# A hybrid layer on one core: K and Q left unnormalised, their norms folded into per-token factors

## The reference, cut to what matters

```
mixed = silu(causal_conv4(x @ w_qkv));  q, k, v = split(mixed)      # 16 heads of q, k; 32 of v
q = q * rsqrt(sum(q*q) + 1e-6) * 128 ** -0.5
k = k * rsqrt(sum(k*k) + 1e-6)
state = state * exp(g_t)                                            # per head, 128 x 128
delta = (v_t - k_t @ state) * beta_t
state = state + outer(k_t, delta);   out_t = q_t @ state
core = norm_w * (out * rsqrt(mean(out*out) + 1e-6)) * silu(z);      result = core @ w_out
```

## Time and profile before

| | |
|---|---|
| median of 3 runs | 4429.54 us (4429.43 to 4431.3) |
| the profiled execution, its time | 4427.73 us |
| its span, first to last instruction | 4426.0 us |
| mean granted clock of PE | 0.984 |
| busy, share of the span | PE 96%, DVE 77%, ACT 52%, POOL 10% |

### The profile page before, as it was taken

One profiled execution on the slowest core, in us unless ns is written; L12 is line 12 of the kernel. 1 busy time (PEld: TensorE's weight loads), 2 busy tenths in 40 slices (PEclk: granted clock), 3 DMA queues, 4 the chain that ended last, 5 costly groups with the idle time before them and its releaser, 6 DMA issues. The chain is left out here.

```text
span 4426.0 us, 80007 instructions
## 1 busy us (share of the span) xinstructions
PE 4253.2 (96%) x29877; PEld 2612.2 (59%) x29877; DVE 3409.0 (77%) x8579; ACT 2317.5 (52%) x4857; POOL 433.1 (10%) x342
## 2 busy tenths in 40 slices
PE   7899999999999999999999999998699999999898
PEld 4566666666666666666666666666344444444443
DVE  5888888888888888887888888786345989898950
ACT  4555555555555555555555555554244545564542
POOL 1111111111111111111111111110000000000000
PEclk9999999999999999999999999999899999999999
DMA  2111111111111112111111110100203445454520
GB/s 73 41 37 37 32 39 32 32 35 37 32 39 32 34 33 70 44 34 32 37 33 34 42 32 30 37 30 11 90 1 99 149 140 161 147 162 136 174 83 10
DMA packets 202405, 263.32 MB, mean 59 GB/s; under 512 B 18175, under 2 KB 101379, under 8 KB 202019
## 3 DMA queue, kind: packets, MB, share of 16 engines
q1 hardware_dynamic: 202018, 258.20, 18.3%
HBM read 249.24 MB, written 8.91 MB: 58 GB/s over the span
## 5 line engine op out<-in xcount | busy, mean ns | idle before, releaser
L455 PE MATMUL bank<-xnT,w_qkv 128*128 128x512 f32 x2048 | 928.2, 596 | 4.1 <-ACT raw L738 3.4
L455 PEld LDWEIGHTS bank<-xnT,w_qkv 128*128 128x128 f32 x2048 | 374.9, 192 | 403.9 <-issue 385.2
L1028 DVE SCALAR_TENSOR_TENSOR conv<-raw,conv_w,conv 128x1024 f32<-128x1024 f32 x384 | 495.4, 1290 | 125.8 <-ACT conv L715 116.6
L568 PE MATMUL bank<-w_out_unit,oT 128*128 128x512 f32 x1024 | 504.8, 616 | 7.9 <-ACT oT L783 7.9
L529 PE MATMUL bank<-w_z_unit,xnT 128*128 128x256 f32 x2048 | 487.5, 381 | 0.0
L529 PEld LDWEIGHTS bank<-w_z_unit,xnT 128*128 128x128 f32 x2048 | 371.8, 192 | 41.1 <-issue 1.0
L1240 PE MATMUL bank<-xnT_f,w_gu 128*128 128x512 f32 x704 | 326.5, 608 | 5.0 <-ACT xnT_f L1697 4.1
L814 ACT ACTIVATE squares<-o 128x128 f32<-128x128 f32 x512 | 153.9, 301 | 322.8 <-DVE o L1072 261.6
L1258 PE MATMUL bank<-w_down,hidden 128*128 128x512 f32 x704 | 318.6, 596 | 1.9 <-DVE x_blocks L1300 1.9
L1248 PE MATMUL bank<-xnT_f,w_gu 128*128 128x512 f32 x704 | 317.7, 594 | 0.0
L655 ACT ACTIVATE q_state<-bank,e_gc 128x128 f32<-128x128 f32 x448 | 139.9, 363 | 239.1 <-PE bank L440 230.3
(11 more groups left out here) (228 smaller groups left out, 8113.3 us busy)
## 6 DMA issues: line engine op xcount, KB each, us to landing
rows_b<-bc_rows SPq DMA_DIRECT2D x256, 256.0 KB, 3.4
rows_c<-bc_rows SPq DMA_DIRECT2D x256, 256.0 KB, 3.5
w_qkv<-in_w_qkv SPq DMA_DIRECT2D x128, 256.0 KB, 2.9
decay<-gc_rows SPq DMA_DIRECT2D x64, 512.0 KB, 3.9
w_z_unit<-in_w_z SPq DMA_DIRECT2D x32, 512.0 KB, 4.4
w_out_unit<-in_w_out SPq DMA_DIRECT2D x32, 512.0 KB, 5.0
x_after<-x SPq DMA_DIRECT2D x16, 256.0 KB, 2.0
x_blocks<-x_after SPq DMA_DIRECT2D x4, 1024.0 KB, 11.5
```

The lines of the kernel that those rows point to most:

```text
L455: made = e.matmul(PROJ[:, :], w_qkv[:, p % 2, j, :], xnT[:, n // HK, j, h * BANK:(h + 1) * BANK], start=j == 0, stop=j == KT - 1)
L568: made = e.matmul(OB[:, :], oT[:, r, :], w_out[:, N % 2, r, :], start=r == 0, stop=r == REP - 1)
L1028: e.scalar_tensor_tensor(acc, raw[:, i % 2, tap:tap + T], conv_w[:, tap, col:col + 1], acc, ALU.mult, ALU.add).then_inc(on["conv"], 1)
```

## The change

K and Q stay as silu leaves them. Their norms are needed only as one number for each token, and these are put where a factor for each token is applied anyway:
- PE sums the squares in 16 matmuls whose weights are 32 columns of ones. Each takes the 128 tokens of one chunk and writes 32 partitions of the bank, so all 2 x 1024 sums lie in one bank. ACT copies the bank to `norm_rows` (the buffer of K's squares), PE turns it in four transposes, so that tokens lie on partitions, and ACT takes one logarithm of 128x16 and three exponentials of 128x8 (`norms`).
- K: the column that is subtracted from `decay` has the logarithm of K's sum added (`col_beta`, DVE), and V is scaled by the root of K's sum when it is evicted (`evict_v`: four activations with a scale for each token, in place of one copy).
- Q: its factor goes into the output's scale: POOL multiplies the sums of squares of the output by 1 / sum (`q_square`), before the logarithm, and the inverse root by Q's factor (`q_factor`).
- In `scalar` the exponentials of `decay` and the logarithm and exponential of the output scale stand later in their slot, behind the copies of u and of the turned o. The first half of `decay` is subtracted and selected in slot 8 (was 5) and its exponential is in slot 8 (was 7); the second half keeps slots 9 and 11.

```diff
@@ -310,8 +315,8 @@
                 if pair == 1:
                     e.wait_ge(on["a_weight"], 4 * N + 2 * a + 1)
                 elif a == 0:
-                    e.wait_ge(on["kq_norm"], 2 * N + 2)
-                    e.wait_ge(on["ln"], 4 * N + 4)
+                    e.wait_ge(on["silu"], 4 * N + 2)
+                    e.wait_ge(on["ln"], N + 1)
                 else:
                     e.wait_ge(on["v_evict"], 4 * N + 4)
                 for i in range(2):
...
 
-            def sums(n, p, h):
-                N = n
-                e.wait_ge(on["square"], 2 * N + p + 1)
-                if p or h:
-                    e.wait_ge(on["ln"], 4 * N + 2 * p + h)
-                elif n > 0:
+            def sums(N):
+
+                e.wait_ge(on["square"], 2 * N + 2)
+                if N > 0:
                     e.wait_ge(on["a_weight"], 4 * N)
-                sq = conv[:, (4 * N + p) % 3, h * BANK:(h + 1) * BANK]
-                e.matmul(MIX[:, :], c["ones"][:, :], sq, start=True, stop=True).then_inc(on["sums"], 1)
+                for p in range(2):
+                    sq = conv[:, (4 * N + p) % 3, :]
+                    for h in range(2):
+                        for j in range(4):
+                            t, lo = 4 * h + j, (2 * p + h) * P
+                            made = e.matmul(MIX[32 * j:32 * j + 32, lo:lo + P], c["ones"][:, 0:32],
+                                            sq[:, t * P:(t + 1) * P], start=True, stop=True)
+                made.then_inc(on["sums"], 1)
+
+            def turn_sums(N):
+                e.wait_ge(on["ss_copy"], N + 1)
+                for i in range(4):
+                    made = e.transpose(MIX[:, i * P:(i + 1) * P], norm_rows(N)[:, i * P:(i + 1) * P], c["ident"][:, :])
+                made.then_inc(on["ss_turned"], 1)
 
             def turn_v(n, group):
...
 
+                n = unit_at_only(slot, 6)
+                if n is not None:
+                    sums(n)
                 for p in range(2):
-                    n = unit_at_only(slot, 6 + p)
...
 
+                n = unit_at_only(slot, 6)
+                if n is not None:
+                    turn_sums(n)
                 for p in range(2):
-                    n = unit_at_only(slot, 6 + p)
...
@@ -583,11 +598,21 @@
 
         def scalar(e):
 
-            def log_of_sum(n, p, h):
-                N = n
-                e.wait_ge(on["sums"], 4 * N + 2 * p + h + 1)
-                sq = conv[:, (4 * N + p) % 3, h * BANK:(h + 1) * BANK]
-                e.activation(sq, MIX[:, :], ACT.Ln, bias=c["eps"]).then_inc(on["ln"], 1)
+            def norms(N):
+
+                e.wait_ge(on["ss_turned"], N + 1)
+                by_token = MIX[:, :].rearrange("p (i t w) -> p i t w", i=2, w=32)[:, :, :, 0]
+                e.activation(ln_norm[:, N % 3, :, :], by_token, ACT.Ln, bias=c["eps"]).then_inc(on["ln"], 1)
+                e.wait_ge(on["ln"], N + 1)
+                if N > 0:
+                    e.wait_ge(on["v_evict"], 4 * N)
+                e.activation(v_scale[:, :], ln_norm[:, N % 3, K, :], ACT.Exp, scale=0.5).then_inc(on["norm_exp"], 1)
+                if N >= 3:
+                    e.wait_ge(on["o_scaled"], 2 * (N - 2))
+                e.activation(q_square[:, N % 3, :], ln_norm[:, N % 3, Q, :], ACT.Exp, scale=-1.0).then_inc(
+                    on["norm_exp"], 1)
+                e.activation(q_factor[:, N % 3, :], ln_norm[:, N % 3, Q, :], ACT.Exp, scale=-0.5,
+                             bias=c["q_scale"]).then_inc(on["norm_exp"], 1)
 
             def evict_v(n, group):
                 N = n
@@ -595,8 +620,12 @@
                 e.wait_ge(on["v_turned"], 4 * N + group + 1)
                 if n >= 2:
                     e.wait_ge(on["resid"], LINKS * (N - 2) + 4 * q + 3)
-                e.copy(v_tok[:, N % 2, 4 * q:4 * q + 4, r, :],
-                       MIX[:, :].rearrange("p (i w) -> p i w", w=P)).then_inc(on["v_evict"], 1)
+                e.wait_ge(on["norm_exp"], 3 * N + 1)
+                for i in range(4):
+                    t = 4 * q + i
+                    made = e.activation(v_tok[:, N % 2, t, r, :], MIX[:, i * P:(i + 1) * P], ACT.Copy,
+                                        scale=v_scale[:, t:t + 1])
+                made.then_inc(on["v_evict"], 1)
 
...
 
             for slot in range(ATTENTION_SLOTS):
+                n = unit_at_only(slot - 1, 6)
+                if n is not None:
+                    norms(n)
                 for p in range(2):
-                    n = unit_at_only(slot - 1, 6 + p)
-                    if n is not None:
-                        log_of_sum(n, p, 1)
                     n = unit_at_only(slot - 1, 10 + p)
...
-                        N = n
-                        e.wait_ge(on["select"], 2 * N + a + 1)
-                        dec = decay_half(N, a)
-                        e.activation(dec, dec, ACT.Exp).then_inc(on["decay_exp"], 1)
-                for p in range(2):
-                    n = unit_at_only(slot, 7 + p)
-                    if n is not None:
-                        N = n
-                        e.wait_ge(on["ln"], 4 * N + 2 * p + 2)
-                        sq = conv[:, (4 * N + p) % 3, :]
-                        e.activation(sq, sq, ACT.Exp, scale=-0.5, bias=c["q_scale"] if p == Q else 0.0).then_inc(
-                            on["norm_exp"], 1)
-                n = unit_at_only(slot, 24)
-                if n is not None:
-                    N = n
-                    e.wait_ge(on["squares"], 8 * N + 8)
-                    square_sum = o_rstd[:, N % 2, :, :]
-                    e.activation(square_sum, square_sum, ACT.Ln, bias=c["eps"], scale=1.0 / DK).then_inc(
-                        on["rstd_ln"], 1)
-                    e.wait_ge(on["rstd_ln"], N + 1)
-                    e.activation(square_sum, square_sum, ACT.Exp, scale=-0.5).then_inc(on["rstd"], 1)
                 for i in range(4):
                     n = unit_at_only(slot, 2 + 2 * i)
...
                         if i == K and n > 0:
-                            e.wait_ge(on["kq_norm"], 2 * N)
+                            e.wait_ge(on["sums"], N)
                         elif i == Q and n > 0:
                             e.wait_ge(on["v_turned"], 4 * N - 1)
                         elif i == V0 and n > 0:
                             e.wait_ge(on["v_turned"], 4 * N)
                         elif i == V1:
-                            e.wait_ge(on["kq_norm"], 2 * N + 1)
+                            e.wait_ge(on["ss_turned"], N + 1)
                         if p == 0:
...
 
+                n = unit_at_only(slot, 6)
+                if n is not None:
+                    e.wait_ge(on["sums"], n + 1)
+                    e.copy(norm_rows(n), MIX[:, :]).then_inc(on["ss_copy"], 1)
...
                         on["oT_copy"], 1)
+
+                for a in range(2):
+                    n = unit_at_only(slot, (8, 11)[a])
+                    if n is not None:
+                        N = n
+                        e.wait_ge(on["select"], 2 * N + a + 1)
+                        dec = decay_half(N, a)
+                        e.activation(dec, dec, ACT.Exp).then_inc(on["decay_exp"], 1)
+                n = unit_at_only(slot, 24)
+                if n is not None:
+                    N = n
+                    e.wait_ge(on["o_square"], N + 1)
+                    square_sum = o_rstd[:, N % 2, :, :]
+                    e.activation(square_sum, square_sum, ACT.Ln, bias=c["eps"], scale=1.0 / DK ** 2).then_inc(
+                        on["rstd_ln"], 1)
+                    e.wait_ge(on["rstd_ln"], N + 1)
+                    e.activation(square_sum, square_sum, ACT.Exp, scale=-0.5).then_inc(on["rstd"], 1)
 
                 n, t = unit_at(slot, ZPROJ)
...
                         evict_pair(n, a, 0)
-                for p in range(2):
-                    n = unit_at_only(slot, 7 + p)
+                for a in range(2):
+                    n = unit_at_only(slot, 8 + a)
                     if n is not None:
                         N = n
-                        e.wait_ge(on["norm_exp"], 2 * N + p + 1)
-                        vec = kq[:, N % 3, p, :]
-                        e.tensor_tensor(vec, vec, conv[:, (4 * N + p) % 3, :], ALU.mult).then_inc(on["kq_norm"], 1)
+                        if a == 0:
+                            if N in (0, HK):
+                                e.wait_ge(on["gates"], 2 * (N // HK) + 2)
+                            e.wait_ge(on["ln"], N + 1)
+                            if N > 0:
+                                e.wait_ge(on["decay_sub"], 2 * N)
+                            norm = ln_norm[:, N % 3, K, :].unsqueeze(1).broadcast_to([P, REP, NC])
+                            heads = slice(REP * (n % HK), REP * (n % HK + 1))
+                            e.tensor_tensor(col_beta[:, :, :], gc_beta[:, n // HK, heads, :], norm, ALU.add).then_inc(
+                                on["col_beta"], 1)
```

(62 more changed lines are left out.)

4 lines of the change are left out of this document (removed).

## The result

The changed kernel takes 4383.29 us (median of 4 runs, 4372.25 to 4385.94) against 4429.49 us before: a ratio of 0.9892, 95% interval 0.9877 to 0.9907. Faster by 1.1%, inside the range given, 14 us above the predicted time. The profiled execution took 4372.25 us (span 4370.5), 55.5 less than that of before. That profile and the median stand 11 us apart, and this is most of the 14 us that the prediction was off.

The account below looks back on a forecast made before the run. PE's stream was taken as the bound: 3.44 - 1.1 - 0.44 = 1.9 us less a unit, 61 us over 32 units, less 1 to 2 at the start, 59.5; 4369 us forecast, range 4358 to 4400.

Parts of the forecast that it names:

- The bound: Between about 200 and 2900 us the time is what PE has to stream; PE busy 2199.08 of 2200 us.
- the tiles' overlap: The 16 sums' matmuls in four column groups run nearly fully side by side: 0.86 us, 1.1 with changes of form.
- rival A: The forecast as worked out, with nearly full overlap of the column tiles: 4369 us, own range 4358 to 4380; chance 0.72.
- B: Column tiles overlap only in part, weight loads not beside streams on the same rows: 1.9 us, 4396 in all; chance 0.12.
- C: Column tiles run one after the other: 3.64 us for the 16 sums, 4451 us in all, slower than before; chance 0.07.
- The unit: One key head of a batch element, 8 slots: from 94.49 to 92.6 us, 1.9 us less, 32 units.
- The start: In the first unit PE waits for v's longer evictions on ACT: 1 to 2 us lost, once.
- rival D: A new PE wait, likeliest for resid in slot 7 or the turned sums' copy; 0.6 us a unit gives 4388; chance 0.09.
- DVE ... stays at 81%: DVE's load in the steady stretch, after losing two norm multiplications of 1.23 us each and gaining one small one.
- POOL and ACT take one such duration each: Slot 8: POOL's selection and ACT's exponential each last like DVE's subtraction, some 3.7 us for the three.
- the 8 us: Reserve between the end of the first-half decay exponential in slot 8 and its first reader on PE in slot 9.
- The second half runs as before and begins earlier: The part of the kernel from 3030 us on keeps its duration and only starts sooner.

## Why the prediction was right, and where it was off

- *The bound, and the tiles' overlap (rival A)*: held. The 16 sums with their two changes of form take 1.17 us, forecast 1.1; as 16 serial ones they take 3.57 (forecast 3.44). The factor is 3.5. B (1.9 us) and C (3.64) fell with that, and the condition of B, a weight load that cannot run beside a stream over the same rows, fell with it: four matmuls of 128 rows start within 21 ns, again every 109 ns, though one of their weight loads lasts 109 ns by itself (below, from the groups of 700 to 2900 us). The Trainium skill's rule (TensorE: Matmul & The Clock Gate, Part 3, "The mechanism") that loads overlap only when row_grp differs does not describe this; the measurement decides. The Trainium skill's figure for three column tiles (the same page, "Measured speedup vs the span model"), stretched to four, gave by the prediction's estimate about 1.1 us for the 16 without the changes of form; 1.01 were measured.

```profile
L339 PEld LDWEIGHTS bank<-conv,ones 128*32 128x32 f32 x768 | 19.5, 109 | 2.9
```

- *The unit*: 92.66 us, forecast 92.6. The saving was 1.83 instead of 1.9 us, 2 us over 32 units.
- *The start*: mis-sized. 1 to 2 us were taken for v's evictions, and their two waits did grow by 1.1 us; but 3.2 us were lost in all, the largest new wait being that for the state's copy behind the subtraction and the taps in slot 8 of the first unit. It is of rival D's kind, at a place that D did not name, in the one unit where DVE has no reserve. The start and the unit make up the 4 us between the forecast 59.5 and the 55.5 of the profiled pair. Some of this is luck: the profile after had 10 us less at 1.2 GHz in its start than that of before, and the two traces with as much as before lost 3.8 and 5.2 us.
- *"DVE ... stays at 81%" and the relief of no value*: right for the time, wrong as a reading. The relief isn't spare. With 1.66 us of idle work in the place of each multiplication the unit takes 1.17 us more, 37 us in all; with the 1.23 us that were taken out it would be less, but by the reserve of 0.88 us in slot 8 not nothing.
- *"POOL and ACT take one such duration each"*: low for POOL; 2.00 us for the selection in slot 8 instead of 1.23, because DVE's additions run beside it. Hidden in the 8 us.
- *"The second half runs as before and begins earlier"*: this step failed. It holds for 4 of 12 executions. The others take some 7 to 14 us longer, and these make the median; in the two of them that left a trace the time is in this part and in the start, with PE longer at 1.2 GHz. The prediction had only one profile of before to go by, and gave the half-clock stretches of its partly idle stages no width of their own, and 9 us (0.2%) to the measurement where 12 executions spread over 18.6. The median, 4383.29, lies outside A's own range (4358 to 4380). The whole range covered it because it had been drawn for B and D, which did not come: that part is luck. What decides which pattern an execution takes is open.

## What to carry to other kernels

When PE is the bound, cost an edit by the distance from one group's start to the next; here that gave the unit to 0.1%. Matmuls with few output rows can be worth putting in column tiles (3.5 times here, for four), if consecutive matmuls go to different tiles; tiled groups should stand together. Work taken off an engine that is not the bound can still be what a moved instruction stands on: look which slot has under 1 us of reserve before calling the relief worthless. And where part of the span runs at a changing clock, one profile does not give the median to better than that part's spread.

## What the runs showed of the hardware

- The order of the same 16 matmuls (128 rows, 32 columns, 128 streamed) sets their time: 1.01 us over four tiles in turn, 2.39 us tile by tile. At full width they take 3.57 us.
- In the tile-by-tile order the next tile's first matmul starts 466 ns behind the first of the tile ahead, while three of its eight records have still to start.
- Going from whole-array to tiled matmuls and back costs 0.10 + 0.06 us. With tiled groups side by side about 0.15 us of it is saved.
- A selection on POOL and additions over 128x1024 on DVE slow each other: 2.00 against 1.09 us for the one, 4.66 against 3.92 for three of the others.
- The same instructions in a stretch that PE does not fill took 1477.0 to 1488.5 us on one core, with 112 to 136 us of it at 1.2 GHz.
